# Spreading the router's bisection steps evenly over the last head group of an attention and mixture-of-experts kernel

## Time and profile before

| | |
|---|---|
| Median of three runs | 2432.1 us |
| The three runs | 2432.11, 2432.1, 2405.56 us |
| Profiled execution, its own time | 2422.2 us |
| Span of its trace | 2420.5 us |
| Mean granted clock of TensorE | 0.968 |
| Busy: PE / DVE / ACT / POOL | 96% / 80% / 62% / 10% |

### The profile page before, as it was taken

How to read it: one execution, slowest core, us unless ns; L and a number is a source line. 1 busy time by engine, 2 the same in 40 slices (tenths; PEclk the granted TensorE clock), 3 DMA queues, 4 the chain that set the end, 5 groups by cost and what they waited for, 6 DMA issues and landing times. The chain is left out here.

```text
span 2420.5 us, 52762 instructions
## 1 busy us (share of the span) xinstructions
PE 2326.6 (96%) x20275; PEld 1509.8 (62%) x20275; DVE 1929.3 (80%) x3721; ACT 1495.1 (62%) x2901; POOL 242.1 (10%) x228
## 2 busy tenths in 40 slices
PE   7987999999999999999999999998998999999997
PEld 4554555455555555555555555557887888888886
DVE  6776999999999898999999999954744666666664
ACT  2234667788877777788888887663223545454543
POOL 3000000000000000000002000001120222322232
PEclk9957999999999999999999999979999999999999
DMA  7854000004000005100001000002242445344444
GB/s 261 319 155 86 17 11 10 4 11 79 13 8 11 14 18 101 30 13 11 9 4 41 4 4 4 30 4 70 86 158 86 125 133 138 96 122 133 138 102 117
DMA packets 141914, 167.97 MB, mean 69 GB/s; under 512 B 53612, under 2 KB 107372, under 8 KB 141628
## 3 DMA queue, kind: packets, MB, share of 16 engines
q1 hardware_dynamic: 127916, 142.87, 19.4%
q0 software_dynamic: 13728, 22.28, 5.0%
q10 hardware_dynamic: 64, 0.02, 0.0%
HBM read 117.86 MB, written 48.56 MB: 69 GB/s over the span
## 5 line engine op out<-in xcount | busy, mean ns | idle before, releaser
L957 DVE TENSOR_REDUCE a_mp<-a_pm 128x1 f32<-128x512 f32 (+3 forms) x2176 | 1293.7, 665 | 84.9 <-PE a_pm L1124 54.0
L1082 ACT ACTIVATE a_p<-a_ps 128x512 f32<-128x512 f32 (+2 forms) x2176 | 1122.3, 586 | 384.5 <-PE a_ps L1205 270.7
L1227 PE MATMUL a_po<-a_p,a_v 128*32 128x384 f32 (+2 forms) x8688 | 619.4, 388 | 0.9
L1124 PE MATMUL a_pm<-a_k,a_q 48*128 48x512 f32 (+3 forms) x1152 | 411.8, 440 | 5.1
L1124 PE MATMUL a_pm<-a_k,a_qr 48*128 48x512 f32 (+3 forms) x1152 | 411.9, 455 | 3.0 <-ACT p_xs L379 1.2
L1205 PE MATMUL a_ps<-a_qr,a_k 50*128 50x512 f32 (+3 forms) x1152 | 388.3, 432 | 22.6 <-DMA a_qr<-a_nb 22.6
L1205 PE MATMUL a_ps<-a_q,a_k 50*128 50x512 f32 (+3 forms) x1152 | 379.9, 430 | 0.0
L1227 PEld LDWEIGHTS a_po<-a_p,a_v 128*32 128x32 f32 x8688 | 203.6, 110 | 203.0 <-issue 136.1
L1205 PEld LDWEIGHTS a_ps<-a_qr,a_k 50*128 50x128 f32 x1152 | 191.9, 191 | 205.1 <-ACT a_p L1082 150.8
L1205 PEld LDWEIGHTS a_ps<-a_q,a_k 50*128 50x128 f32 x1152 | 189.3, 189 | 182.4 <-ACT a_p L1082 157.3
L1647 ACT ACTIVATE e_g<-e_pg 128x512 f32<-128x512 f32 x128 | 76.6, 599 | 243.0 <-PE e_pu L1725 243.0
(11 more groups left out here) (183 smaller groups left out, 1946.6 us busy)
## 6 DMA issues: line engine op xcount, KB each, us to landing
e_wgu<-in_wg SPq DMA_DIRECT2D x18, 1024.0 KB, 5.6
e_wgu<-in_wu SPq DMA_DIRECT2D x18, 1024.0 KB, 7.5
e_wd<-in_wd SPq DMA_DIRECT2D x18, 1024.0 KB, 10.3
q_parts<-p_parts SPq DMA_DIRECT2D x16, 512.0 KB, 5.7
k_parts<-p_parts SPq DMA_DIRECT2D x16, 512.0 KB, 6.6
a_k<-k_parts SPq DMA_DIRECT2D x60, 128.0 KB, 3.7
a_q<-q_parts SPq DMA_DIRECT2D x96, 64.0 KB, 2.3
a_qr<-q_parts SPq DMA_DIRECT2D x84, 64.0 KB, 2.4
```

The source lines that it names most:

```text
L957: eng.tensor_reduce(mp[:, i, heads[0]:heads[-1] + 1, r, kc], ps[:, 0:len(heads) * w].rearrange("p (a n) -> p a n", n=w), AX.X, ALU.max).th ...
L1082: eng.activation(pr[:, i, heads[0]:heads[-1] + 1, off:GT], pS[n % HEADS][:, 0:len(heads) * w].rearrange("p (a n) -> p a n", n=w), ACT.Exp) ...
L1124: last = eng.matmul(ps[:, n * w:(n + 1) * w], QT[t % SLOTS][tile, a, r * P:(r + 1) * P], KT[g % 2][tile, a, kc * GT:kc * GT + w], start=n ...
L1227: last = eng.matmul(pO[h * VW:(h + 1) * VW, lo:hi], V[TILES[t][0] % 2][:, b, h * VD:h * VD + VW], PR[blk % PBUF][:, h, lo:hi], start=b == ...
```

## The change

The 32 bits keep their order and their work. Before, four of them were placed in tile 25, five in tile 26, eight in tile 27 and fifteen in tile 28, evenly within each. Now they are placed evenly from window 559 to window 692, one for each 4.3 stretches (windows), from tile 24 to tile 28. `spread`, `limit` and the `slot` items keep their places.

```
@@ plan() @@
             others[BEGIN[LAST - 7] + 8].append(("spread", 0))
-            b = 0
-            for t, count_of in ((LAST - 6, 4), (LAST - 5, 5), (LAST - 4, 8), (LAST - 3, 15)):
-                for m in range(count_of):
-                    others[BEGIN[t] + (2 * m + 1) * (BEGIN[t + 1] - BEGIN[t]) // (2 * count_of)].append(("bit", b))
-                    b += 1
-            assert b == BITS
+            lo, hi = BEGIN[LAST - 7] + 13, BEGIN[LAST - 2] - 2
+            for b in range(BITS):
+                others[lo + b * (hi - lo) // BITS].append(("bit", b))
             others[BEGIN[LAST - 2] + 2].append(("limit", 0))
```

## The result

| | median | lowest to highest | runs |
|---|---|---|---|
| before | 2429.49 us | 2404.9 to 2455.32 | 20 |
| changed | 2412.47 us | 2407.94 to 2416.73 | 20 |

The ratio is 0.9952, with a 95% interval of 0.9931 to 0.9973: faster, by some 0.5%. That is less than the 2% that the prediction took as what a measurement can tell, but the interval lies clear of 1. The ratio leaves out runs over 1.5% above the fastest of their kernel, here the three slowest of the kernel before; between the medians of all runs the difference is 17.0 us, 0.7%. The forecast was 2412. The spread says more than the medians: the runs of the changed kernel lie within 9 us, those of the kernel before within 50.

What follows compares the result with a forecast made beforehand. TensorE sets the pace at 1.87 us a window, VectorE beyond some 97.5% busy. Terms for tiles 24 to 29 sum to -15.0 us: 2422.2 to 2407.2, plus half of 9.9, 2412 us; range 2387 to 2434.

Steps and rivals of the forecast that it cites:

- tile 28: Ten bits fewer, nine units more: 38.5 us against 56.12, so -17.6 us, of which 10.1 are the clock's.
- tile 29: Its first 9.23 us at half clock would take 5.9, and three more units cost 0.2: -3.1 us.
- The 7.5 us for the queue of bits: Part of tile 28's 17.6 us saving not due to the clock: 7.5 us lost to bits queueing on VectorE.
- Tile 24: Eight bits more, ten units fewer: +4.0 us, ends +1.0 and +5.0; 79 to 82 us long, DVE busy over 97%.
- The GpSimd term: In tile 24, a bit's candidate operation (L524) beside GpSimd's split lasts 1.72 us, not 0.16: 1.6 us more for VectorE.
- Tile 25: Four bits more, seven units fewer: +2.5 us, other end +0.4; VectorE has room.
- the price of a bit by its spacing: A bit costs 0.18 us nine windows apart, 0.43 at six, 0.47 at three; 0.45 taken at the new 4.3.
- The step from the sum to the median: Runs' median lies 9.9 us above the profiled execution; half of that added to 2407.2 us gives 2412.
- The first rival: The clock falls near 1570 us whatever the bits do: sum -1.6 us, time 2426 us, chance 0.20.
- The second: Rival: VectorE overloaded in tiles 24 and 25 brings the clock down there: +13 us, time 2440 us, chance 0.10.
- The fourth: Rival: units pile up in tile 28 where bits leave; some 42 us there, sum -11; within the forecast's shared 0.70.
- The third: Rival: saturation harmless, bits at 0.18 us throughout, about 7 us off: -22, time 2405 us; within the forecast's shared 0.70.

Runs made afterwards that it cites:

- e7: Kernel before, bits as they are, with three products of zeros ahead of each of tile 28's fifteen bits: 2411.95 us, ratio 0.9941.
- 66 repeats: The kernel before, unchanged, run 66 times over three batches: 52 have a mean clock below 0.970; the 8 at 0.973 and more have median 2409.3 us.
- e6: Changed kernel with 24 of its 32 bits left out, the other eight placed evenly over the same windows, for timing alone: 2398.63 us.
- e2: Changed kernel with fifteen bits placed densely, 1.33 windows apart, in tile 26, eight ahead and nine behind, four windows or more apart: 2435.28 us, ratio 1.0074.
- e5: Kernel before with the fifteen bits of tile 28 left out, the other 17 as before: 2403.26 us, ratio 0.989.
- e10: The changed kernel run once more, unaltered, on the same chip: 2412.31 us.
- e3: Kernel before with the next part's first tokens loaded 20 windows later, so GpSimd's split no longer lies beside the fifteen bits: 2424.36 us, ratio 0.9998.
- e8: Changed kernel with its bits placed evenly from window 587 to 703, none in tile 24, and `limit` and the slots later: 2414.14 us.
- e1: Kernel before with eight of the fifteen bits of tile 28 moved to tiles 25 to 27: 2410.12 us, ratio 0.9939.
- e9: Changed kernel with its bits placed evenly from window 587 to 693, none in tile 24: 2411.01 us.

## Why the prediction was right

- **The place and the sum.** The sum of -15.0 us met -14.1 in tiles 24 to 30. The two terms that carry it, tile 28 (-17.6) and tile 29 (-3.1), came out at -17.2 and -3.4. The division of tile 28 by its clock was what made them hold: 13.4 us of the sum were the clock's. e7, as fast as the changed kernel with its bits still dense, and the 66 repeats show that the clock is the whole of the gain.
- **The 7.5 us for the queue of bits** were given back almost wholly. Without the clock the forecast nets to -1.6 us; by the repeats at full clock it is 0 to +3. Spreading the bits over tiles with a busy VectorE costs as much as their queue did. One reading under this term was wrong: the 3.77 us in which PE is idle ahead of 1569 us are not in part waits for PSUM buffers. By name 3.15 us are waits for counts and 0.53 us is the wait of the transpose for `max` on VectorE (L962). And since idle time is only half of the 7.5 us, the other half is longer busy time of TensorE.
- **Tile 24** was set 1.8 us too high. The GpSimd term was wrong in size: the candidate's operation beside GpSimd's split lasted 0.30 us in place of 0.16, not 1.72, since it met only the end of one of GpSimd's casts. VectorE's busy time, 79.4 us in the forecast with this term, came out at 75.16, 95% of the tile; the sign of over 97% did not come, nor the L524 of over 1 us. VectorE and GpSimd in order of time, changed kernel:

```profile
1307.37 0.30 DVE L524 TENSOR_TENSOR r_cand<-r_th,r_bit 128x1 int32<-128x1 int32 x1
...
1306.62 1.04 POOL L939 CAST a_k<-a_k 128x1024 fp32r<-128x1024 f32 x1
```

- **Tile 25** was set 1.9 us too low, tiles 26 and 27 by 0.9 and 1.3. The step that failed is the price of a bit by its spacing. By the prediction's own working a bit costs in tile 25, 71.87 - 36 x 1.870 + 18 x 0.05 = 5.5 us for 8, 0.68 each; tiles 24, 26 and 27 give 0.39, 0.58 and 0.67, at one and the same spacing of 4.3 windows. The mean over all tiles by e6 is 0.50, so the 0.45 held as a mean and in no single tile. Nor is it mostly a wait: of the 4.4 us that tile 25 gained 3.7 are busy time of TensorE (71.13 against 67.42), and the products for the bits sum to only 1.7 us more. The rest fits fewer products running side by side, but no run tests that; what sets the price of a tile stays open.
- **Tile 30** had no term. It became 1.5 us shorter, because the short fall of the clock at 1630 us is not there. In none of the ten experiments' traces does that tile last over 16.8 us, so the fall was no fixed part of the kernel, and its going is luck, not the change's work. What brought it down in a stretch with PE busy stays open.
- **The step from the sum to the median** was right by number only, which is luck. Half of the 9.9 us was added for what might lie elsewhere. That the median of before stood above its profiled execution by time at half clock follows from the line through the repeats; that this time lay in the mended stretch is inferred from how close the changed kernel's repeats lie. So the whole 9.9 us went, and the forecast met the median because the 5 us that had been added for it came from other places: they are 2.2 us ahead of tile 24, 1.0 behind attention, 1.0 in the sum, and 1.0 between the changed kernel's own profile and its median.
- **The first rival** is refuted for the fall at 1569 us by e2, e5 and e7; the fall at 1630 us, which it also built on, has no explanation. **The second** did not come in the profile, but its mechanism is real: e2 shows a fall in tile 25 at this change's density, and e10 has one run in twelve with a lower clock.
- **The fourth** held in part: nine units did come back to tile 28, without harm, VectorE being busy 32.30 us where 32.8 was worked out, and TensorE's waits for `r_ge` are gone there, as was named. **The third**, bits at 0.18 throughout, did not come; its 7 us is also too small a sum, since 0.27 less for each of 32 bits is 8.6.

## What to carry to other kernels

When the repeats of a kernel spread by 1 to 2% and the mean clock goes with them, look for the stretch in which TensorE waits for a short queue on another engine; here the waits themselves were 4 us and the half clock behind them cost 13. Spread such a serial chain so that no stretch puts the other engine over its bound. Here the gain was in the clock alone, and the cost of the steps was paid again wherever they went. Before pricing a move by the queue that it dissolves, compare the kernel's own runs at full clock with those below it: that difference, 20 us here (2429.5 against 2409.3), is what the clock can give.

## What the runs showed of the hardware

- The clock fell behind waits of 1.45 us (e2), 0.5 us twice (e3) and, in the kernel before, five within 20 us of which the longest was 1.77. It then stayed at 0.50 for 17 us (1412 to 1429 in e2), 34 us (1569 to 1603 in the kernel before), 44 us (1467 to 1511 in e2) and 48 us (1564 to 1612 in e3), with PE busy all the time. What sets the length these runs do not show.
- Such a wait does not always bring a fall. Behind the 1.77 us at 1552 us in the kernel before the clock held 1.00 for 16 us, and in e8 TensorE was busy only 0.88 of the 2 us from 1414 us, with the clock at 1.00 throughout tiles 22 to 31.
- One fall of the lengths seen does not make the spread of 50 us. The slowest runs of the kernel before (2455 us at 0.951) have some 110 us more at half clock than those at 0.973, an estimate from (1 - clock) x 2 x time; so they hold several falls or longer ones, and no such run was profiled.
- One us at half clock costs this kernel 0.39 us, by the line through the repeats, and not 0.5. That other engines pace part of each window would explain it, but was not tested.
- Products of zeros, three in 0.66 us ahead of a wait, kept the clock at 1.00 and were worth more than they cost: 49.61 us in tile 28, against 56.12 at a mean clock of 0.78.
- Single runs of nearly every placement (e1, e8, e9, e10) have a mean clock of 0.964 to 0.967 and are 13 to 20 us slower than their median. The changed kernel has such a run once in 32. They were not profiled, so where their clock fell is not known.
